# Projection and FFN of a fused vision-attention-FFN kernel as three float32r products, and the last step's cell sum moved from TensorE to VectorE

## What is computed

```python
h = h + attention(layernorm(h))        # 16 heads of 16; q and k are layer-normed per head and rotated
                                       # out = concat(heads) @ w_proj.T + b_proj
x = layernorm(h)
base   = x @ W_lin.T + b_lin
scores = softmax(x @ gate_w.T)         # 8 experts, the best 2 are kept
lora   = sum over the 2 experts of weight * (x @ left[e]) @ right[e]
h = h + base + lora
```

## Time and profile before

| | us |
|---|---|
| median of 3 runs | 750.31 |
| lowest and highest | 746.08 to 753.61 |
| the profiled execution: its time | 748.84 |
| the profiled execution: span from the first to the last instruction | 747.1 |

### The profile page before, as it was taken

How to read it: one execution, slowest core, us unless ns; L and a number is a source line. 1 busy time by engine, 2 the same in 40 slices (tenths; PEclk the granted TensorE clock), 3 DMA queues, 4 the chain that set the end, 5 groups by cost and what they waited for, 6 DMA issues and landing times.

```text
span 747.1 us, 23721 instructions
## 1 busy us (share of the span) xinstructions
PE 692.7 (93%) x9277; PEld 556.3 (74%) x9277; DVE 531.6 (71%) x1204; ACT 394.9 (53%) x969; POOL 422.0 (56%) x450
## 2 busy tenths in 40 slices
PE   5998998999976889999999999999999999999884
PEld 3987887888754667788788778778778787877652
DVE  2468687878883367787887877887878878866642
ACT  4553543535332256656666665656666565665431
POOL 3667572764657246567566575575575575663221
PEclk9999999999997699999999999999999999999976
DMA  8963562330110122223223223223222322122100
GB/s 220 235 155 114 148 199 47 81 69 28 38 42 16 31 70 69 64 71 74 78 72 75 83 70 77 80 68 78 78 72 71 83 74 73 41 58 56 37 19 27
DMA packets 69524, 58.69 MB, mean 79 GB/s; under 512 B 30607, under 2 KB 68646, under 8 KB 69286
## 3 DMA queue, kind: packets, MB, share of 16 engines
q1 hardware_dynamic: 69414, 57.18, 29.9%
HBM read 33.69 MB, written 11.40 MB: 60 GB/s over the span
## 4 chain that ended last, share of the span: by engine, by line
PE 73%; DVE 14%; issue 3%; ACT 3%; DMA 3%; SPq 2%; POOL 1%; POOLq 0%; DVEq 0%; ACTq 0%
PE p_a L1331 13%; PE p_c L1331 11%; PE p_s L1391 6%; PE p_o L1403 6%; PE p_conv L758 6%; PE p_kv L758 5%; PE p_c L1451 4%; PE p_s L1373 3%; PE p_n L1411 3%; PE p_mm L758 3%; PE p_a L1357 2%; PE p_s L1387 2%; PE p_c L1432 2%; DMA kr<-qkT 2%; DVE kv L656 2%
## 5 line engine op out<-in xcount | busy, mean ns | idle before, releaser
L1126 POOL TENSOR_TENSOR t<-t,ss_rs 116x512 f32<-116x512 f32 x48 | 50.9, 1060 | 126.4 <-ACT ss_rs L1173 125.2
L1266 DVE TENSOR_REDUCE mx<-p_s 87x16 bf16<-87x1392 f32 x64 | 101.6, 1587 | 24.6 <-PE p_s L1373 24.3
L1197 ACT ACTIVATE prT<-p_s 87x1392 f32<-87x1392 f32 x64 | 85.1, 1329 | 57.8 <-PE p_s L1391 56.3
L426 POOL TENSOR_TENSOR xs_lo<-xcols,xs_hi 120x585 fp32r<-120x585 f32 (+1 forms) x45 | 60.4, 1350 | 43.8 <-ACT xs_hi L483 43.8
L1120 POOL TENSOR_TENSOR t<-t 116x512 f32<-116x512 f32 x48 | 61.0, 1270 | 18.0 <-DVE t L1257 18.0
L1391 PE MATMUL p_s<-qr,kr 32*87 32x87 f32 x2048 | 67.9, 255 | 0.0
L1129 POOL TENSOR_TENSOR t<-t,tabs 116x512 f32<-116x512 f32 x48 | 62.9, 1310 | 3.8
L1391 PEld LDWEIGHTS p_s<-qr,kr 32*87 32x87 f32 x2048 | 59.5, 152 | 0.0
L1387 PE MATMUL p_s<-mxT,pick_row 32*87 32x87 bf16 x1024 | 55.4, 207 | 1.4 <-ACT mxT L1191 1.4
L1331 PE MATMUL p_c<-w_f,yT 128*116 128x296 f32 x184 | 56.0, 427 | 0.4 <-ACT yT L1216 0.4
L1403 PE MATMUL p_o<-prT,vp 87*32 87x87 f32 x2048 | 54.7, 246 | 0.0
(11 more groups left out here) (267 smaller groups left out, 1896.6 us busy)
## 6 DMA issues: line engine op xcount, KB each, us to landing
xcols<-in_x_cols SPq DMA_DIRECT2D x12, 822.7 KB, 8.0
h<-h_tokens SPq DMA_DIRECT2D x16, 348.0 KB
out<-out_sb SPq DMA_DIRECT2D x48, 116.0 KB
h_tokens<-in_txt SPq DMA_DIRECT2D x4, 1232.0 KB, 8.7
x<-in_txt_cols SPq DMA_DIRECT2D x32, 154.0 KB, 3.2
qr<-qkT SPq DMA_DIRECT2D x64, 58.0 KB, 2.2
kr<-qkT SPq DMA_DIRECT2D x64, 58.0 KB, 2.0
vp<-vt SPq DMA_DIRECT2D x32, 87.0 KB
```

What stands on the lines that cost most here:

```text
L426: nc.gpsimd.tensor_tensor(xs.lo[:, n % XS_SLOTS, :, 0:M].bitcast(F32R), raw, xs.hi[:, n % XS_SLOTS, :, 0:M], ALU.subtract).then_inc(S['xs_ ...
L1126: link(nc.gpsimd.tensor_tensor(t4, t4, ss_rs[:, b].unsqueeze(2).broadcast_to([TP, 2 * HEADS, HD]), ALU.mult))
L1197: nc.scalar.activation(prT[:, k % 2], p_s[0:SEQ, :, 0:QUADS * SEQ], ACT.Exp, scale=HD ** -0.5).then_inc(S['s_exp'], 1)
L1266: nc.vector.reduce_max(mx[:, k % 2, :, 0:QUADS], p_s[0:SEQ, :, 0:QUADS * SP].rearrange("p j (a k) -> p j a k", k=SP)[:, :, :, 0:SEQ], AX_X ...
```

## The change

- `w_proj` and the FFN's weights are split once into hi (ScalarE, in group 0's `rstd_a`) and lo (GpSimd, in group 0's `hb.1`). `proj` and `ffn` become `mm_split`.
- `oB` and `yT` copy twice out of PSUM: as float32 into a new buffer of two slots, and as float32r into the hi part. New steps `oB_lo` (four a group, 128 partitions x 174) and `yT_lo` (three a group, 128 x 232) subtract the two on GpSimd. `proj` and `ffn` wait for these.
- The gate's exponential is taken as three ScalarE instructions that subtract the maximum by their bias; VectorE's subtraction goes.
- The last step's cells are added by VectorE as in the other steps, and `aggT` is two transposes. What waited for that step's `aggT` (group 0's first `exp` and `hb`) waits for `agg`.
- All five tables of the second stage are written anew, with a period of 276 in place of 288. Among it: token rows are loaded at -440 and read by `stats.0` at -202 (before: -500 and -397); `stats` of group 1 stands behind the last patch step's `att` on VectorE; on TensorE the last step's `aggT` stands before group 0's `qkT.1` (before: behind it).

The core of the diff (buffers, semaphore names and three of the tables left out):

```diff
-                if name == 'sum' and s < STEPS - 1:
+                if name == 'sum':
...
-                    if s < STEPS - 1:
-                        pe_.wait_ge(S['agg'], s + 1)
-                        transpose(p_T, agg[0:M], M).then_inc(S['aggT'], 1)
-                    else:
-                        pe_.wait_ge(S['vw'], PIECES * (s + 1))
-                        for c in range(CC):
-                            part = slice(C + P * c, C + P * (c + 1))
-                            mm_ = mm(p_T[:, c, 0:M], [kv[0:M, ring(s, j), i, part] for j in range(PIECES) for i in range(LOAD_CELLS)]
-                                     + [bias_kv[0:1, part]], [ident[0:M, 0:M]] * CELLS + [consts.ones[0:1, 0:M]])
-                        mm_.then_inc(S['aggT'], 1)
+                    pe_.wait_ge(S['agg'], s + 1)
+                    transpose(p_T, agg[0:M], M).then_inc(S['aggT'], 1)
...
+GROUP_PE = table("""qk.0.-48 qk.1.19 v.0.84 qkT.0.131 qk.2.148 qkT.1.194 v.1.211 qkT.2.277 peak.0.281 mT.0.315 scores.0.325
+                peak.1.353 mT.1.378 scores.1.388 pv.0.412 peak.2.419 mT.2.444 scores.2.453 oN.0.475 peak.3.482
+                pv.1.497 mT.3.520 pv.2.522 scores.3.529 oN.1.548 oB.0.569 oN.2.587 oB.1.611 pv.3.622 oB.2.651
+                oN.3.674 oB.3.715 proj.0.722 proj.1.739 yT.0.756 yT.1.771 proj.2.838 ffn.0.869 ffn.1.890
+                yT.2.911 ffn.2.932 twT.0.1072 lora.0.1092 lora.1.1232""")
+GROUP_POOL = table("""xc.0.-264 xlo.0.-86 add.0.33 scale.0.63 shift.0.110 add.1.153 scale.1.166 shift.1.177 add.2.220 scale.2.249
+                shift.2.260 hb.0.571 oB_lo.0.599 hb.1.582 oB_lo.1.683 oB_lo.2.688 oB_lo.3.768 hb.2.612
+                yT_lo.0.856 yT_lo.1.880 yT_lo.2.925 base.0.931 above.0.969 base.1.1036 base.2.1070""")
...
-GROUP_PERIOD, GROUP_START = 288, 2100
+GROUP_PERIOD, GROUP_START = 276, 2100
...
+                if name == 'oB_lo':
+                    pool.wait_ge(S['oB_out'], GB * g + k + 1)
+                    if k == 0:
+                        wait(pool, S['proj'], 3 * (g - 1))
+                    part = (slice(None), half, slice(None), slice(SEQ * k, SEQ * (k + 1)))
+                    nc.gpsimd.tensor_tensor(onT.lo[part].bitcast(F32R), on_raw[:, k % 2], onT.hi[part],
+                                            ALU.subtract).then_inc(S['oB_low'], 1)
+                if name == 'yT_lo':
+                    pool.wait_ge(S['yT_out'], 3 * g + k + 1)
+                    wait(pool, S['ffn'], 3 * g + k - 1)
+                    nc.gpsimd.tensor_tensor(yT.lo[:, b].bitcast(F32R), y_raw[:, b], yT.hi[:, b], ALU.subtract).then_inc(S['yT_low'], 1)
...
+                    if g == 0 and k == 1:
+                        for n, (w, raw) in enumerate(((wp, w_p), (wf, w_f))):
+                            pool.wait_ge(S['w2_high'], n + 1)
+                            nc.gpsimd.tensor_tensor(w.lo[:].bitcast(F32R), raw[:], w.hi[:], ALU.subtract).then_inc(S['w2_low'], 1)
...
+                    if g == 0:
+                        act.wait_ge(W['agg'], STEPS - 1)
+                        act.wait_ge(W['kv_mm'], CONVS)
+                        act.wait_ge(consts.w_in, 16 * consts.LOADS)
+                        act.wait_ge(consts.S['w_sub'], 3 * CC)
+                        nc.scalar.copy(wp.hi[:].bitcast(F32R), w_p[:]).then_inc(S['w2_high'], 1)
+                        nc.scalar.copy(wf.hi[:].bitcast(F32R), w_f[:]).then_inc(S['w2_high'], 1)
...
-                    nc.scalar.copy(onT[:, half, :, SEQ * k:SEQ * (k + 1)],
+                    wait(act, S['oB_low'], n4 - 2)
+                    nc.scalar.copy(on_raw[:, k % 2], p_n[:, 0:CC * SP].rearrange("p (c q) -> p c q", c=CC)[:, :, 0:SEQ])
+                    nc.scalar.copy(onT.hi[:, half, :, SEQ * k:SEQ * (k + 1)].bitcast(F32R),
...
+                    wait(act, S['yT_low'], n3 - 2)
+                    nc.scalar.copy(y_raw[:, b], product('tile', g, k)[:, 0:CC * TP].rearrange("p (c n) -> p c n", c=CC))
+                    nc.scalar.copy(yT.hi[:, b].bitcast(F32R), product('tile', g, k)[:, 0:CC * TP].rearrange("p (c n) -> p c n", c=CC)).then_inc(S['yT_out'], 1)
...
-                    nc.scalar.activation(g_e[:], g_e[:], ACT.Exp).then_inc(S['g_exp'], 1)
+                    act.wait_ge(S['ffn_out'], 3 * g + 3)
+                    wait(act, S['tw_ok'], g)
+                    for tile in range(TILES):
+                        last = nc.scalar.activation(g_e[:, tile], f[:, half, tile, C + LR:FFN_N], ACT.Exp, bias=g_max[:, tile:tile + 1])
+                    last.then_inc(S['g_exp'], 1)
...
-                    pe.wait_ge(S['oB_out'], GB * g + min(k + 1, GB - 1) + 1)
-                    mm(product('tile', g, k)[0:TP, 0:C], [onT[:, half, c, TP * k:TP * (k + 1)] for c in range(CC)],
-                       [w_p[:, c] for c in range(CC)]).then_inc(S['proj'], 1)
+                    pe.wait_ge(S['oB_low'], GB * g + min(k + 1, GB - 1) + 1)
+                    mm_split(product('tile', g, k)[0:TP, 0:C], onT.chunks(lambda x_, c: x_[:, half, c, TP * k:TP * (k + 1)]),
+                             wp.chunks(lambda x_, c: x_[:, c])).then_inc(S['proj'], 1)
...
-                    pe.wait_ge(S['yT_out'], n3)
-                    mm(product('tile', g, k)[0:TP, 0:FFN_N], [yT[:, b, c] for c in range(CC)], [w_f[:, c] for c in range(CC)]
-                       ).then_inc(S['ffn'], 1)
+                    pe.wait_ge(S['yT_low'], n3)
+                    mm_split(product('tile', g, k)[0:TP, 0:FFN_N], yT.chunks(lambda x_, c: x_[:, b, c]), wf.chunks(lambda x_, c: x_[:, c])
+                             ).then_inc(S['ffn'], 1)
```

50 lines of the change are left out of this document (21 added, 29 removed).

## The result

| | before | after |
|---|---|---|
| median, us (19 runs each) | 750.31 (743.69 to 756.32) | 740.62 (731.72 to 749.08) |
| ratio, 95% interval | | 0.9854 (0.982 to 0.9888) |
| span of the profiled execution, us | 747.1 | 734.0 |
| first scores of the first group (`p_s<-kr,qr`) | 259.6 | 248.0 |
| of the second group | 286.3 | 279.6 |

The change gives 1.5%, 10 to 11 us, where 22 were forecast. Medians are of all runs; the ratio leaves out those more than 1.5% above the fastest of their kernel (6 of the 19 after the change). The profiled execution gives 13.1, and the table tells where they are: 11.6 us at the first scores, of which only 6.7 are left one group later; 9.5 more over the fourteen steps to the last group (0.68 a step); and 3.1 lost again in the drain.

A forecast was written before the change was run, and what follows sets the result against it. TensorE's own work was taken to bound the kernel for some 370 us. Products -13, passage -11 and drain +2 made -22, from 748.84 to 727 us profiled, 728 us as the median; range 715 to 742.

The forecast's parts named there:

- Passage: Between the stages: summing the last step's cells on VectorE, with earlier shifts and statistics, saves 11 us (7 to 14).
- Groups: Steady groups: six float32r matmuls per projection or FFN product save 0.87 us a group, 13 us over 15 groups.
- I take no hole in the steady groups: TensorE gets no new wait in steady groups; a possible 5 us in all is kept for the range.
- the thinnest place: Before `ffn.2`: 2.0 us needed against 2.1 of cover; if ScalarE is late, a hole of some 0.3 us a group.
- By the line between the two, 296 columns cost 0.90 us: FFN product: six float32r matmuls priced between 0.80 us at 256 columns and 1.47 at 512; 0.13 us saved a tile.
- qkT.0: TensorE's wait for `shift.0`, queued behind `yT_lo.2`: 2.1 us between them, `shift` takes 1.3, so 0.8 are left.
- about as tight as before: Order of `kr`'s placing DMAs against `peak.0`: the same 2 us or so stay, up or down.
- Drain: End of the kernel: longer chain of copies and subtractions, partly offset by shorter products; net 2 us lost (0 to 4).
- Start only: Rival, 16 in 100: cover before `ffn.2` and `qkT.0` is missed, groups stay at 28.7 us; 741 us.
- products only: Rival, 14 in 100: the passage stays late behind SP's queue or the last step's copies; 738 us.
- GpSimd was never the bound: Rival, 6 in 100: 4.2 us of new subtractions lengthen each group to 32.9 us; about 808 us, half of it 774.
- The four passes: Rival, 12 in 100: three products against float32's four passes save the full quarter, 20 us in groups; 721 us.

The follow-up runs named there:

- old_sum: The changed kernel with only the last step's sum put back on TensorE as its 40 matmuls; 746.4 us, ratio 0.9958 to the kernel before.
- f32_products: The changed kernel with projection and FFN products put back to plain float32, double copies, low parts and tables kept; 751.4 us, ratio 1.0034 to the kernel before.
- order5: The changed kernel with VectorE's h2.0 ahead of the third tile's rotation and TensorE's oN.2 between first FFN product and scores; 738.0 us, ratio 0.9811.
- six_old_order: The kernel before with the last step's sum on VectorE and six float32r matmuls per product, old tables, low parts missing; 734.9 us, ratio 0.9804.
- lows_dve: The changed kernel with the last group's seven low parts on VectorE instead of GpSimd; 742.5 us, ratio 0.9873 to the kernel before.

## Why the prediction was wrong

The time fell inside the range given, but the change gave less than half of what was forecast. By medians 12.3 of the 22 us are missing. The profiled execution lacks 8.9 of them, which are placed below; the other 3.4 are the distance of the medians from the profiled executions (4.9 us for the changed kernel, 1.5 before), and no trace shows where they lie.

**Passage: 11 us forecast, 11.6 at the first scores, 6.7 after one group.** VectorE's two sums ended at 234.6 (forecast 237.5), `proj` started at 239.1 (238.5), first scores at 248.0 (near 248.5). The step that failed is that a start 11 us earlier was counted as 11 us at the end. The passage's first scores now stand in a stretch where TensorE waits for VectorE and ScalarE (0.28, 0.49, 1.46 and 0.75 us between 250 and 257 us), and its clock halves right behind, from 258.9 to 272.5. Filling those waits kept the first group free of the fall in all six kernels that had the extra matmuls. The earlier trace rows had shown the half clock in the passage, and the forecast read it as a property of the slow sum and not as something that could move into the first group. That the first scores came to within 1 us of the forecast is in part luck. The 9.3 us that it took off were 40 matmuls at half clock; they take 5.5 in old_sum, and the sum is worth only 3.2 us at the first scores with the new tables and 5.5 with the old ones, while kernels with the same sum and the new tables have their first scores anywhere between 246.6 and 252.3. The rest of the 11.6 came with the tables and with the moments at which the clock changed.

**Groups: 0.87 us a group forecast, 0.56 in the lowest step and 0.65 in the mean.** The price of the products was right: 0.88 in the old order, 0.95 from f32_products to the changed kernel (6.36 and 5.41), 0.90 of it in the step. The step that failed is "I take no hole in the steady groups". There were two. The wait for `h` costs 0.26 us a group (1.31 against 1.05 in all eleven groups compared), and order5, which takes it away, gets 0.20 back. The other is at the thinnest place that the forecast named: `ffn.2` waits about 0.16 us for `yT_lo.2` in every steady group. The forecast set 2.0 us of need against 2.1 of cover; its own terms add to 2.07 (0.4 + 0.70 + 0.67 + 0.3), and the steps in between take 1.87 (0.19 + 1.49 + 0.15 + 0.04) while 2.02 pass from the start of `yT.2` to that of `ffn.2`. No run takes this wait away, so its price is read from the trace alone. Beside these, the forecast took a product's price for its own. "By the line between the two, 296 columns cost 0.90 us" is what a product takes behind `mT` and ahead of `oN` (0.90 in order5); behind `qk` or `v` and ahead of `mT` it takes 0.81 (six_old_order), and the three in the new tables, ahead of 32-row or 32-column matmuls, take 0.98. The earlier trace rows showed it: the 0.87 has `qkT` ahead and `oN` behind, the 1.05 has peaks ahead and `pv` behind. But this cost only changed places, as the table at f32_products shows.

**Cover.** `qkT.0` held. The hole for `h` came at a place that the forecast did not cost, a bank that is read by an instruction late in VectorE's queue. It took nothing for what small gains uncover, either. six_old_order shows this most plainly: it saved 0.88 in the products, and 0.2 of it went at once to the transposed maxima. And the order of `kr` against `peak.0` is not "about as tight as before": from the landing to the first scores of a group 1.2 to 1.4 us passed in nine of the sixteen groups before, and 0.14 to 0.6 pass in all after the first now. A smaller misreading: the earlier trace rows's second stretch, 462 to 492 us, is one of the three slower groups, so not all between 318 and 607 us are alike.

**GpSimd and the low parts** were right: 595 and 679 ns measured (0.55 and 0.67), 22.4 us a group, no bound. So was ScalarE.
```profile
L1130 POOL TENSOR_TENSOR onT_lo<-on_raw,onT_hi 128x174 fp32r<-128x174 f32 x4 | 2.3, 595 | 1.1 <-issue 1.1
...
L1135 POOL TENSOR_TENSOR yT_lo<-y_raw,yT_hi 128x232 fp32r<-128x232 f32 x3 | 2.0, 679 | 2.4 <-issue 2.4
```
These answer: groups of instructions of one steady group.

**Drain: 2 us forecast, 3.1 measured, and more than that in most runs.** Kernels with the old tables took 59.5 to 60.8 us from the last group's first scores to the end, those with the changed tables and float32r products and the steps left as they are 62.6 to 66.9. From the last FFN product to the end it is 13.9 to 15.9 us in all of these, so the loss lies ahead of it. That product starts 44.2 to 45.0 us behind the last group's first scores with the old tables and 47.8 to 53.0 with the new, the last projection product 36.6 before (724.15 - 687.57) and 41.1 after (712.48 - 671.36). The forecast's cause, the longer way of copies and low parts, is there: the last FFN product waits 1.73 us where it waited 0.73. The rest goes with the order: the new tables keep more of a group behind the first scores of the next, and at the end nothing covers it. The forecast let 1 us of that show. No run takes this alone, so it stays argued; and how much of the spread is TensorE's clock, which in these kernels falls at different moments of the drain, stays open too.

**The rivals.** "Start only" (741 us) names the time measured, and "products only" (738) one near it, but neither happened as told: in the profiled execution both gains are there, each cut by something else. "Start only" had one condition right, the missed cover before `ffn.2`. By medians, though, nothing beyond the sum's own 10 us can be seen, and the traces do not say why. GpSimd was never the bound. The four passes: by the forecast's own working, the four passes that the Trainium skill (FP8 and Floating Point Precision, TensorE Precision Notes) gives for true FP32 would have saved 1.4 us a group, and the products saved 0.88 in the old order and 0.95 in the new, so the trace does not bear it out in full for products this short.

## What to carry over

Where TensorE is the bound, cost an operation from its start to the start of what follows, and compare whole groups: a step can get dearer because its neighbours changed while another gets cheaper by the same amount. Idle time in the view is a lower bound, since modelled ends hide short waits; a start at a constant distance behind its producer's end, group after group, gives them away. A stage that starts earlier is worth what is left one stage later; look at what the clock did on either side of the old wait, and at where the waits that it hid come out. When all engines run fixed orders, first count the least time of each loop through them (2.22 us from peaks to transposed maxima, 2.02 from `yT.2` to `ffn.2` here), since a saving past that is handed to the next wait.

## What the hardware showed that I had not expected

- A step that stands right ahead of matmuls on 32 rows or 32 columns takes 0.09 us more from its start to theirs, in all three kinds of step that can be compared, and one behind them takes more too: `oN` 0.44 and 0.53, the float32 projection behind `qkT` 0.87 and 0.96, six float32r matmuls of 296 columns behind `mT` 0.89 and 0.98; `oN` ahead of `mT` 0.44 behind `qk` and 0.51 behind `pv`. Moving another step in between moved the cost to that step.
- TensorE's granted clock fell to 1.2 GHz in the first group of all nine kernels with the new tables and no extra matmuls, for 10 to 24 us in seven of them and 3.4 in two. In the changed kernel it had waited a quarter of the 11 us before, and stayed at 1.2 GHz through 13.6 us in which it was busy for 12.89. Eleven unused matmuls kept it at 2.4 GHz through the first group; in three of those six kernels 3.4 us at 1.2 GHz came right behind it.
- The landing of `kr` is a tie with the first scores in half of the steady groups of the changed kernel (0.14 us from landing to start) and now and then much later: the last group of lows_dve waited 2.94 us for it.
